# A two-layer transformer kernel on one core: set-up loads on two queues, composed weights made in the second body, and one accumulator for two groups of heads

## The reference, cut to what matters

```
xn = layernorm(x)
x = x + L0_attn(xn) + L0_ffn(xn)
xn = layernorm(x)
x = x + L1_attn(xn) + L1_ffn(xn)
# L0_attn: q, k from xh @ maps, rms_norm; softmax(q k^T * scale + causal) @ v; out @ W_O, for each of 16 heads
# L0_ffn:  sigmoid(xr @ W_r) * (relu(xk @ W_k)^2 @ W_v), xr and xk mix a row with the row before it
# L1_attn: qkv = x @ w_qkv; softmax(q k^T * scale + phi_bias) @ v; @ w_proj + b_proj
# L1_ffn:  W1, W2 = sum_k softmax(logits)_k * A_k @ B_k   (32 primitives of rank 64);  gelu(x @ W1) @ W2
```

## Time and profile before

| | before |
|---|---|
| median of 3 runs | 1824.24 us (1821.36 to 1831.1) |
| the profiled execution: its time | 1823.52 us |
| the profiled execution: its span | 1821.7 us |
| PE busy | 1622.6 us, 89% of the span |
| DVE busy | 1469.0 us, 81% |
| ACT busy | 1322.1 us, 73% |
| POOL busy | 942.4 us, 52% |

### The profile page before, as it was taken

How to read it: one execution, slowest core, us unless ns; L and a number is a source line. 1 busy time by engine, 2 the same in 40 slices (tenths; PEclk the granted TensorE clock), 3 DMA queues, 4 the chain that set the end, 5 groups by cost and what they waited for, 6 DMA issues and landing times.

```text
span 1821.7 us, 33616 instructions
## 1 busy us (share of the span) xinstructions
PE 1622.6 (89%) x11850; PEld 640.0 (35%) x11850; DVE 1469.0 (81%) x2653; ACT 1322.1 (73%) x2566; POOL 942.4 (52%) x1144
## 2 busy tenths in 40 slices
PE   4798898888889888889999999999999999999995
PEld 2453343333333333333332333323333233333331
DVE  4358878888888788888879888998889888898881
ACT  1227777776777677677778888888888788888875
POOL 2124555555555555455455556655565555564555
PEclk9759999999999999999999999999999999999999
DMA  8312323232322323323222322232222321222200
GB/s 269 58 40 61 68 63 65 62 66 62 71 71 70 67 71 63 71 74 72 59 53 59 59 58 52 46 70 59 58 52 45 71 58 54 48 54 62 61 14 18
DMA packets 133126, 116.41 MB, mean 64 GB/s; under 512 B 16856, under 2 KB 125664, under 8 KB 132960
## 3 DMA queue, kind: packets, MB, share of 16 engines
q1 hardware_dynamic: 126272, 100.64, 24.7%
q0 software_dynamic: 4096, 8.40, 1.4%
q10 hardware_dynamic: 2592, 5.24, 0.9%
HBM read 79.63 MB, written 33.55 MB: 62 GB/s over the span
## 4 chain that ended last, share of the span: by engine, by line
PE 46%; DVE 22%; ACT 10%; issue 7%; POOL 7%; DMA 5%; SPq 2%; DVEq 0%; POOLq 0%; ACTq 0%
PE pv_acc L627 14%; PE scores_transposed L643 10%; ACT probs L937 6%; DVE maxs L1144 4%; PE scores_transposed L771 4%; DMA stacks<-parts_scratch 4%; PE scores_for_max L664 3%; DVE maxs L1147 3%; DVE xn L1067 2%; DVE maxs L1175 2%; POOL x_between_layers L1231 2%; PE scores_transposed L743 2%; PE scores_for_max L779 2%; SPq L478 2%; PE scores_for_max L693 1%
## 5 line engine op out<-in xcount | busy, mean ns | idle before, releaser
L937 ACT ACTIVATE probs<-scores_transposed 128x512 f32<-128x512 f32 x1664 | 919.3, 601 | 214.4 <-PE scores_transposed L643 206.8
L643 PE MATMUL scores_transposed<-stacks 62*128 62x512 bf16 (+3 forms) x2048 | 581.4, 347 | 50.6 <-ACT probs L937 34.4
L1309 POOL TENSOR_TENSOR probs<-probs,near_bias 128x512 f32<-128x512 f32 x256 | 325.1, 1274 | 370.1 <-ACT probs L937 369.8
L627 PE MATMUL pv_acc<-probs,vals 128*32 128x512 f32 (+3 forms) x4096 | 474.8, 536 | 7.8 <-POOL probs L1283 3.8
L1144 DVE TENSOR_REDUCE maxs<-scores_for_max 128x2 f32<-128x1024 f32 x322 | 388.1, 1220 | 78.1 <-PE scores_for_max L664 76.8
L643 PEld LDWEIGHTS scores_transposed<-stacks 62*128 62x128 bf16 x2048 | 153.6, 94 | 618.5 <-ACT probs L937 303.8
L664 PE MATMUL scores_for_max<-stacks 60*128 60x512 bf16 x1024 | 336.3, 385 | 18.1 <-DVE maxs L1144 8.7
L1147 DVE TENSOR_REDUCE maxs<-scores_for_max 128x1 f32<-128x512 f32 x380 | 250.6, 682 | 25.7 <-PE scores_for_max L664 22.6
L668 PE MATMUL scores_for_max<-stacks 60*128 60x512 bf16 (+3 forms) x1024 | 255.1, 315 | 9.8 <-DMA stacks<-parts_scratch 8.0
L1283 POOL TENSOR_SCALAR_AFFINE_SELECT probs<-probs 128x512 f32<-128x512 f32 x256 | 175.4, 700 | 151.1 <-ACT probs L937 150.9
L1175 DVE TENSOR_REDUCE maxs<-scores_for_max 128x1 f32<-128x512 f32 x256 | 174.9, 683 | 90.3 <-PE scores_for_max L680 86.3
(11 more groups left out here) (129 smaller groups left out, 2093.1 us busy)
## 6 DMA issues: line engine op xcount, KB each, us to landing
stacks<-parts_scratch SPq DMA_DIRECT2D x768, 64.0 KB
parts_scratch<-parts SPq DMA_DIRECT2D x64, 384.0 KB, 2.6
x_tile<-in_L_attn_x_dram SPq DMA_DIRECT2D x16, 256.0 KB, 2.8
probs<-in_fc_B_dram ACTq DMA_DIRECT2D x1, 4096.0 KB, 19.3
stage_a<-in_fc_A_T_dram SPq DMA_DIRECT2D x1, 4096.0 KB, 16.9
stacks<-mT SPq DMA_DIRECT2D x256, 4.0 KB
x_res<-in_L_attn_x_dram SPq DMA_DIRECT2D x16, 256.0 KB, 3.6
x_tile<-x_between_layers SPq DMA_DIRECT2D x16, 256.0 KB
```

What stands on the lines that cost most here:

```text
L627: last = mm(acc[32 * j:32 * j + 32, q0:T], vals[:, B.parity(off), kt, G * pu + j, :], probs[:, row, column:column + width], start=(kt == 0 ...
L643: last = mm(st[:, bank, column:column + T - q0], ks[p][rows, h, P * kt:P * kt + P], qs[p][rows, h, q0:T], start=True, stop=True)
L937: fn(probs[:, row, :], st[:, B.use(("st", u, number)).bank, :], ACT.Exp, scale=SCALE).then_inc(s["exp_done"], 1)
L1309: g.tensor_tensor(diag, diag, near_bias[:, kt, :].unsqueeze(1).broadcast_to([P, G, P]), ALU.mult).then_inc(s["emul_pool"], 1)
```

## The change

It has two independent parts.

**Two groups per accumulator.** A head now fills 16 (`ACC`) of the 32 rows it gets: for the second group of a pair the value columns are read 16 columns earlier, so that its sums and values land in rows 16 to 24 of each 32, and both groups add up in one accumulation of eight key blocks. The copy, the four transposes and the reciprocal happen twice in a body (`OA`, `OB`), not four times; the reciprocal takes 32 values a row, not 16, and DVE multiplies twice after each. In layer 0 `OT0` (slot 9), `OT1` (16), `OT2` (40) and `OT3` (49) become `OA` (16) and `OB` (49); in layer 1 slots 6, 20, 36 and 48 become 19 and 48. With it the table moves other pieces, in layer 0: `MIX` 0 to 2, `FR` 5 to 6, `FK` 8 to 9, `XT` 11 to 14, `MT1` 17 to 19, `MT2` 37 to 32; in layer 1: `NORM` 16 to 18, `AT` 24 to 25, `PR` 29 to 30, `VP` 32 to 33.

**First bodies anew.** The small loads stand on two queues (8 maps on SP, 10 others on ACT). The tables for the composed weights are issued by ACT once the small ones have landed. DVE makes `wcat` first, and POOL's clearing of the buffers waits for it. `compose_first` moves to slots 32 to 47 of body -1, `compose_second` to slots 48 to 63, four products a slot. The first 24 stack DMAs are issued by SP (q) and ACT (k) at once, and ACT issues the 4 MB table `fc2_A_T` behind its twelve.

```diff
-    0: {"MT0": (2, 0, 0), "FR": (5, 0, 1), "FK": (8, 0, 1), "OT0": (9, 0, -1), "XT": (11, 0, 2),
+    0: {"MT0": (2, 0, 0), "FR": (6, 0, 1), "FK": (9, 0, 1), "XT": (14, 0, 2), "FV": (15, 0, 1),
...
-                        last = mm(acc[32 * j:32 * j + 32, q0:T], vals[:, B.parity(off), kt, G * pu + j, :],
-                                  probs[:, row, column:column + width], start=(kt == 0), stop=(kt == NT - 1),
-                                  skip_group_check=True)
+                        first = VW * (G * pu + j) - ACC * (pu % PAIR)
+                        last = mm(acc[VW * j:VW * j + VW, q0:T], columns[:, first:first + VW],
+                                  probs[:, row, column:column + width], start=(kt == 0 and pu % PAIR == 0),
+                                  stop=(kt == NT - 1 and pu % PAIR == PAIR - 1), skip_group_check=True)
...
-                            if j == 0 and kt == NT - 1 and B.has(eo):
+                            if j == 0 and kt == NT - 1 and u % PAIR == 0 and B.has(eo):
...
-            for slot, _ in enumerate(body(Body(0, FIRST))):
-                compose_first(slot)
+            run(body(Body(0, FIRST)))
             pe.wait_ge(later_in, 16 * LATER_LOADS)
             for slot, _ in enumerate(body(Body(0, FIRST + 1))):
+                compose_first(slot)
                 compose_second(slot)
...
-            load_for_compose(act, 0)
-            load_for_compose(act, 1)
+            for dst, src in setup_loads:
+                act.dma_start(dst, src).then_inc(setup_in, 16)
+            for dst, src in halves_loads:
+                act.dma_start(dst, src).then_inc(halves_in, 16)
+            act.wait_ge(maps_in, 16 * MAP_LOADS)
+            act.wait_ge(halves_in, 16 * HALVES_LOADS)
+            for n in (0, 1, 3):
+                load_for_compose(act, n)
...
             run(body(Body(0, FIRST)))
             act.wait_ge(setup_pool, 5)
+            act.wait_ge(S[0]["parts_stored"], 32)
+            load_stack_rows(act, S[0], 1, 0)
+            load_for_compose(act, 2)
             run(body(Body(0, FIRST + 1)))
...
             def clear_first_buffers():
+                pool.wait_ge(setup_dve, 3)
                 g.memset(vals[:, 0], 0.0).then_inc(setup_pool, 1)
```

211 lines of the change are left out of this document (116 added, 95 removed), and 15 rows, old and new, of the table WORK_USES.

## The result

The changed kernel took 1832.03 us (median of 20 runs) beside 1825.64 us for the kernel before in the same rounds (20 runs): a ratio of 1.0038, 95% interval 1.0023 to 1.0054. That is 0.4% slower and within 0.5% of no change, where the forecast was 1750 and 0.95 for faster. By its number it is what rival E had at 0.03 (within 0.5%). The profiled execution took 1827.56 us, its span 1825.9.

The account below looks back on a forecast made before the run. PE bounds both layers, layer 0 with a stretch to slot 11 where DVE ends last. Start 18 + 1, layer 0 34, double bodies 5 and layer 1 16 give 74 off 1823.5: 1750 us, range 1724 to 1788.

Parts of the forecast that it names:

- rival E: Whole kernel: the change does nothing, other engines fill in and the start is paid back; within 0.5% (9 us), chance 0.03.
- The step that failed in layer 0: Layer 0, slots 12 to 14: PE can pass them while DVE is at `NORM`, as enough banks of maxima are free.
- the 2.4 us forecast for a body: Layer 0: gain per body, taken from a sum of 2.6; 34 us over 14 bodies, bounds 14 and 49.
- The terms for the two copies and for the DVE pair: Layer 0's chain: copies at 288.52 and 311.03 give 0.3 and 0.5 us, slot 40's DVE pair with its transposes 0.5.
- PE's own work: Removed transposes save PE 1.0 us a body; in layer 0 this alone was the lower bound, 14 us.
- Rival A: Layer 0 keeps DVE's pace: time won at `XT` is spent on a free bank; 14 us instead of 34, 1770, chance 0.2.
- ACT's ten loads (about 0.5 us each): Start: these loads stand ahead of ACT's own work but lie before `XT`, which was put at about 13.7.
- The landing: Start: first stacks land 20 to 22 us after the first issue, at about 59.
- 44 us to body 0: Start: from the stacks' landing to body 0, three slots at half clock included; body 0 at 103, 18 us earlier.
- Rival B: Start: second half of body -1 at half clock, 76 us instead of 44; 1782, chance 0.14.
- a second queue saves only issue time: First stacks: two queues halve the issue but use the same engines; landing gains nothing, by the opposite reading 10 us.
- 1.0 us a body was forecast: Layer 1, 16 bodies alone: gain from PE's removed work, 16 us in all, bounds 0 to 29.

Follow-up runs that it names:

- e6: e4 with layer 0's `XT` transposes issued ahead of slot 14's maximum product: 1800.89 us, ratio 0.9888 to the kernel before.
- f1: The kernel before with two 128 x 512 products of fill ahead of `XT`'s wait for `xn` in layer 0: 1812.51 us, ratio 0.9942.
- g2: The changed kernel, nothing moved, with fill products in layer 0's waits at slots 14 and 44: 1796.08 us, ratio 0.9854 to the kernel before.
- e1: The kernel before with only the pairing of groups (`OA`, `OB`), other slots and start as before: 1821.51 us, ratio 0.9969.
- e11: The changed kernel with three tables (`fc1_A_T`, `fc1_B`, `fc2_B`) issued by SP, not ScalarE: 1818.08 us, ratio 0.9949 to the kernel before.
- f2: The kernel with all mends (1764.14 us), with `fc2_A_T` issued by SP before the stacks: 1769.99 us, ratio 0.9707 to the kernel before.
- e10: The changed kernel with the first composition from slot 0 of body -1, not slot 32: 1817.23 us, ratio 0.9950 to the kernel before.
- f4: f2 with eight products of fill ahead of the wait for the first stacks: 1769.73 us, ratio 0.9713 to the kernel before.
- e12: The changed kernel with all 24 DMAs of the first stacks issued by SP: 1834.27 us, ratio 1.0046 to the kernel before.
- e2: The kernel before with layer 0's new slots alone, four groups' products kept: 1846.91 us, ratio 1.0099.
- e3: The kernel before with the new start alone, both layers' bodies as before: 1834.09 us, ratio 1.0035.
- e7: e1 with two 128 x 512 products of fill ahead of `XT`'s wait for `xn` in layer 0: 1815.15 us, ratio 0.9964 to the kernel before.
- e8: e7 with eight repeats of slot 44's maximum product as fill in layer 0: 1798.65 us, ratio 0.9871 to the kernel before.
- e4: The kernel before with the pairing and both layers' new slots, start as before: 1823.38 us, ratio 0.9979.
- e9: e6 with eight repeats of slot 44's maximum product as fill in layer 0: 1794.08 us, ratio 0.9849 to the kernel before.

## Why the prediction was wrong

**The step that failed in layer 0** is this: "Four banks of maxima were free after slot 6, slots 7 to 13 fill three and a half packs, and `OT0` no longer takes one: yes." Slots 7 to 13 fill not three and a half banks but all four, and slot 14's product, which stands *ahead* of `XT` within its slot, is the first that needs a fifth. It waits for a reduction behind `NORM` and carries `XT` with it. The 1.95 us at `XT` became 1.52 at slot 14, and "PE then reaches `XT` at about 371.5, still waits 1 us" did not come about. e6, with `XT` ahead of that product, gave 1.6 us a body back.

**The size was wrong too.** Of the 2.4 us forecast for a body, 0.5 came at equal clock (f1 and g2). The terms for the two copies and for the DVE pair (0.3, 0.5 and 0.5) came to nothing: the copies' share of the chain is not saved when PE goes on to wait for VectorE at `XT` and for ScalarE at slot 44, and e1 shows those waits growing by just the 0.6 us of the transposes that went. PE's own work, which I had taken for a lower bound of 1.0, was not one, because both removed sets stood right ahead of a wait. Rival A had the mechanism, a free bank of VectorE's on which the time won at `XT` is spent, and it too was priced too high. Rival E had the number and not the reason: the start was paid back, but layer 1 took 11.2 us less, and layer 0's 13 bodies 9.8 more, with the clock as the larger part.

**A term was missing: the clock.** The earlier trace rows shows it, 0.95 in layer 0, and the prediction priced clock at the start alone. I took PE's waits at their own length, while what ran behind them at half clock cost nearly as much again. g2 shows it in the changed kernel: nothing moved, 1.3 us of fill in each of two waits, and a body falls by 3.3 us in the trace.

**The start.** The maps, `xn` in 1.12 us and `XT` at 13.7 were right. "ACT's ten loads (about 0.5 us each)" forgot the three large ones, which took 0.81, 5.82 and 6.51 us of ScalarE's time: 9.1 us of the 17.5 forecast, shown by e11. The landing was put at 21 us behind the issue and took 26.4, since `fc2_A_T` is issued behind the stacks onto the same engines (f2); the prediction had named that as a way to be wrong. Then 44 us to body 0 were 50.5. The groups of PE from 73.5 to 124 in the trace of after:

```profile
L573 PE MATMUL pv_acc<-probs 128*128 128x512 f32 x32 | 20.3, 720 | 0.0
L588 PE MATMUL pv_acc<-vals,stage_a 128*128 128x128 f32 x128 | 18.4, 287 | 0.4 <-issue 0.4
L667 PE MATMUL scores_for_max<-stacks 60*128 60x512 bf16 (+3 forms) x33 | 10.6, 322 | 11.2 <-DMA stacks<-parts_scratch 11.2
L679 PE MATMUL scores_for_max<-causal_halves,ident_halves 64*128 64x128 bf16 (+2 forms) x40 | 6.2, 237 | 0.0
```

The half clock was as forecast (6.5 us of it). Too small were the scores (the last two rows, 16.8 us, some of it at half clock, where I had 10), the 16 products of L573 (20.3 us, some of it at half clock, where I had 14) and the 64 products of L588 with their loads, 0.29 us each where I had 0.22 to 0.25. Rival B, half clock up to body 0, did not come. And the composition behind the landing was dear in itself: 16 products at 0.88 us of PE, the bound there, while PE had stood for 11.2 us ahead of it (e10).

From what the Trainium skill ("DMA: Bandwidth & Descriptors", section "Why a DMA increments its semaphore by 16 and not by 1") says, that a DMA uses as many engines as divide its slowest dimension, the lowest-numbered ones, the prediction took that a second queue saves only issue time. The runs do not decide it. Without a load beside them two queues landed the stacks 19.7 (f2) and 23.1 us (f4) behind the issue, and one queue 15.5 to 24.8 in the nine kernels with the old start, where the issue itself took 8.6 to 9.8 us and not 4.4. With 4 MB beside them it was 26.4 against 33.1 (e12), more than the issue alone unhindered; the run does not show why.

**Layer 1 came out near the forecast, and not for the reason given.** 1.0 us a body was forecast and 1.3 measured in seven bodies, but that is the largest difference of the thirteen traces with these slots; they take 55.9 to 57.0 us a body, most of them about 56.5. Over the whole layer the trace gives some 11 of the 16 us. The removed work alone did not bring it. Kernels without the pairing take 855.6 to 858.7 us for layer 1 (before, e2, e3, f1), with the pairing and the old slots 850.4 to 862.7 (e7, e8, e1), with both 842.7 to 849.6. So the gain came only with `OA` at 19 (20 in e1), `NORM` at 18 and what moved by one slot behind them, moves that the prediction had priced at nothing. Which of them does it, and what they would do without the pairing, no run shows. The double bodies gave nothing (157.6 and 158.7 us for the three) for the 5 forecast; they take 157.6 to 168.6 in the traces of all the kernels, at clocks of 0.89 to 0.96, and no run was aimed at them.

Added up from the profiled spans: body 0's `x_res` issue 4.5 us later, the next 13 bodies 9.8 longer, the double bodies 1.1, layer 1 11.2 shorter: 4.2 us, the spans' difference.

## What to carry to other kernels

Before work is taken off an engine, look for the wait that stands next behind it on that engine: what goes ahead of a wait is handed to the wait, and on TensorE a longer wait can cost the clock as well. Read the granted clock of every stage and not only of the start; where it is below 1.00, a wait of TensorE has a second price, and moving useful work into it (e6, 0.9% over e4) or, failing that, filling it (g2, 1.8% over after) is worth a run. Fill every such wait: with only one of two filled, e7 showed no gain over e1. When a step passes another, list the banks claimed by what stands between them *within* the slot too, and when DMA issues go to a compute engine, give large ones the duration that the trace shows for them and not that of a small one. And before a gain is read from one trace, look at the same stretch in every other trace that has it unchanged: the landing of the stacks and the start of body 0 moved by 9 and 12 us with no edit to them.

## What the runs showed of the hardware

- Short waits of TensorE amid dense work go with half clock (1.2 GHz). Stretches of 3.4 or 6.8 us at 0.50 began beside waits of 1.5 us (slot 14), 1.74 (slot 44) and 2.56 us (`XT` in e1), and beside some of 0.94 (e9). Every second body of f1 had none, with waits of 1.14 and 1.02 us in it. Filling them took the granted clock of ten bodies from 0.96 to 1.00 (e1, e8) and from 0.92 to 1.00 (after, g2). The Trainium skill ("TensorE: Matmul & The Clock Gate", Part 1) tells of a clock that falls after idle stretches; these rows agree in kind, and the waits are shorter than I had looked for.
- At these places 3.4 us of half clock lengthened a body by 0.9 to 1.7 us: 0.9 to 1.5 in e1, 1.25 in e7, 1.5 in f1, 1.7 in after (48.2 beside g2's 46.5).
- A DMA issue can hold its engine's queue for long: 5.82 and 6.51 us for 4 MB and 1 MB right behind other large ones on ScalarE (after), 4.00 and 5.06 on SP (e11), beside 0.81 us for the 1 MB ahead of them and 0.41 for 4 MB behind twelve of 64 KB. 24 issues of 64 KB took 8.6 to 9.8 us alone and 20.5 us with a 4 MB load issued beside them on the other queue (e12).
- 24 DMAs of 64 KB landed 15.5 to 24.8 us behind their issue on one queue in nine executions with the same start, 19.7 and 23.1 us on two; with a 4 MB load beside them 26.4 to 28.5 us on two queues and 33.1 on one.
